# The shift of the first three layer norms computed by GpSimd instead of VectorE, in a decoder layer on one core

## The reference, cut to what matters

```python
def _layernorm(x, axis=-1, eps=1e-05):
    m = jnp.mean(x, axis=axis, keepdims=True)
    v = jnp.var(x, axis=axis, keepdims=True)
    return (x - m) / jnp.sqrt(v + eps)
...
    # end of _L0_xattn_ref: ln2, with a gain and an offset
    return layer_norm(att + decoder_seq, ln_gamma, ln_beta)
...
x = _layernorm(x + _L0_attn_ref(x, ...), axis=-1)             # ln1
x = _layernorm(x + _L0_xattn_ref(ctx_1024, x, ...), axis=-1)  # ln3 around ln2
x = _layernorm(x + _L0_ffn_ref(x, ...), axis=-1)              # ln4
```

## Time and profile before

| what | value |
|---|---|
| median of 3 runs | 441.6 us (441.42 to 441.95) |
| profiled execution, its own time | 443.31 us |
| its span from first to last instruction | 441.6 us |
| DVE busy over the span | 397.1 us (90%) |
| ACT busy | 340.6 us (77%) |
| PE busy | 274.4 us (62%) |
| POOL busy | 147.2 us (33%) |
| stretch of the three norms | 357.4 to 393.6 us of the span |

### The profile page before, as it was taken

The page is one execution under the profiler, slowest core; times in us unless marked ns, Lnnn a source line. Parts: engine busy times, 40 slices in busy tenths (PEclk is TensorE's granted clock), DMA queues, the critical chain, the costliest instruction groups (busy, mean ns, idle before and its releaser), DMA issues.

```text
span 441.6 us, 8251 instructions
## 1 busy us (share of the span) xinstructions
PE 274.4 (62%) x2265; PEld 150.6 (34%) x2275; DVE 397.1 (90%) x1261; ACT 340.6 (77%) x801; POOL 147.2 (33%) x327
## 2 busy tenths in 40 slices
PE   6777988989677733332332333399997886274560
PEld 5754435435222210000000000164444785161550
DVE  5978998778799999999999999959988988988987
ACT  2689985979999964999999999965796846548133
POOL 2400000001000000999999999992000005520020
PEclk9899998999755555555555555599999999579597
DMA  7700000000354441699998999877003200000002
GB/s 266 182 0 2 0 1 1 25 24 27 143 190 169 177 154 71 122 206 203 210 202 203 201 211 200 162 169 134 0 1 86 78 1 2 1 0 1 0 1 96
DMA packets 84254, 43.32 MB, mean 98 GB/s; under 512 B 69095, under 2 KB 74487, under 8 KB 84090
## 3 DMA queue, kind: packets, MB, share of 16 engines
q1 hardware_dynamic: 82650, 42.69, 38.5%
q10 hardware_dynamic: 1568, 0.21, 0.4%
HBM read 7.75 MB, written 1.58 MB: 21 GB/s over the span
## 4 chain that ended last, share of the span: by engine, by line
DVE 55%; PE 15%; issue 15%; ACT 11%; POOL 1%; DMA 1%; ACTq 0%; DVEq 0%; SPq 0%; POOLq 0%
DVE mem L1400 15%; PE ps L487 15%; DVE mem L1145 5%; DVE d_max L1148 5%; DVE mem L1315 3%; DVE mem L1572 3%; ACT mem L931 3%; ACT mem L967 2%; DVE r_now L1144 2%; DVE m L1715 2%; DVE m L1716 2%; DVE row_max L1400 2%; ACT mem L1003 2%; DVE neg_max L1144 2%; DVE m L1148 1%
## 5 line engine op out<-in xcount | busy, mean ns | idle before, releaser
L487 PE MATMUL ps<-mem 64*128 64x256 bf16 (+5 forms) x1180 | 173.7, 345 | 103.8 <-DVE row_max L1400 79.3
L487 PEld LDWEIGHTS ps<-mem 64*128 64x128 bf16 (+3 forms) x1188 | 66.2, 115 | 181.0 <-issue 65.9
L1003 ACT ACTIVATE mem<-mem,neg_max 128x256 f32<-128x256 int16 x256 | 118.2, 523 | 10.9 <-DVE neg_max L1144 8.6
L1400 DVE CUSTOM_DVE_ANT_0 mem<-ps,fold,c 128x256 int16<-128x256 f32 x256 | 108.7, 469 | 0.2 <-DVE fold L1145 0.2
L443 POOL TENSOR_SCALAR mem<-mem,r_now 128x256 int16<-128x256 f32 x176 | 82.0, 486 | 71.3 <-DVE r_now L1144 71.2
L487 PE MATMUL ps<-ones_bf 128*128 128x128 bf16 x766 | 60.6, 240 | 23.4 <-DVE m L1666 8.3
L487 PEld LDWEIGHTS ps<-ones_bf 128*128 128x128 bf16 x766 | 53.9, 109 | 40.0 <-ACT mem L967 11.5
L1315 DVE TENSOR_TENSOR mem<-mem 128x1024 bf16<-128x1024 bf16 x78 | 50.3, 694 | 4.4 <-ACT mem L931 3.0
L1003 ACT ACTIVATION_READ_ACCUMULATOR mem<-mem,neg_max x256 | 47.2, 184 | 0.0
L947 ACT ACTIVATE mem<-ps 128x1024 bf16<-128x1024 f32 x48 | 45.4, 1034 | 2.0 <-PE ps L487 1.0
L1148 DVE TENSOR_REDUCE d_max<-ps 128x1 f32<-128x1024 f32 (+1 forms) x33 | 38.1, 1161 | 2.6 <-PE ps L487 2.6
(11 more groups left out here) (218 smaller groups left out, 375.7 us busy)
## 6 DMA issues: line engine op xcount, KB each, us to landing
mem<-mem SPq DMA_DIRECT2D x64, 256.0 KB, 2.3
mem<-in_L_attn_w_qkv SPq DMA_DIRECT2D x1, 1536.0 KB, 8.7
mem<-in_x SPq DMA_DIRECT2D x4, 256.0 KB, 4.6
mem<-in_x SPq DMA_DIRECT2D x1, 1024.0 KB, 5.6
out<-mem SPq DMA_DIRECT2D x4, 256.0 KB, 2.2
xattn_matrix<-mem SPq DMA_DIRECT2D x1, 512.0 KB
mem<-in_L_attn_w_out SPq DMA_DIRECT2D x1, 512.0 KB, 4.6
mem<-in_L_ffn_W SPq DMA_DIRECT2D x2, 256.0 KB, 5.9
```

Of the source, the lines that this page charges most:

```text
L487: return te.matmul(o_, l_, r_, start=start, stop=stop)
L1003: ins = sc.activation(e_ring[:, u % 4, pos], y_ring[:, u % 4, pos], ACT.Exp, scale=scale_reg, bias=neg_max[:, u % 4, pos:pos + 1], accum_o ...
L1400: ins = ve.tensor_tensor_reduce(y_ring[:, unit % 4, pos], ps[:, bank + pos // 2, (pos % 2) * N:(pos % 2 + 1) * N], shift, col("g_dots"), - ...
```

## The change

The shift of ln1, ln2 and ln3 leaves DVE's list. POOL computes it, as two instructions of 128x4 with a semaphore between them: the product of mean and rsd, then times -1. The twelve pairs are put into POOL's list at the places below. DVE's norm steps, which had no wait of their own for rsd since the shift stood between, now wait for it. The fourth norm keeps its shift on DVE. Nothing else moves.

```diff
+            def rows_of(q):
+                return slice(4 * q, 4 * q + 4)
+
+            def shift_of(name, q):
+
+                pool.wait_ge(ln_sem(name, "rsd"), ln_count(name, q))
+                link(pl.tensor_tensor(nmr[:, rows_of(q)], mv[:, rows_of(q), 0], rsd[:, rows_of(q)], ALU.mult))
+                pl.tensor_scalar(nmr[:, rows_of(q)], nmr[:, rows_of(q)], -1.0, 0.0, ALU.mult, ALU.add)                    .then_inc(ln_sem(name, "shift"), 1)
...
-                    (x1_beta, 0), (x1_beta, 1), (x1_beta, 2), (gamma_n2, 0), (x1_beta, 3), (gamma_n2, 1),
-                    (gamma_n2, 2), (x2_b2, 0), (x2_b2, 1), (gamma_n2, 3), (x2_b2, 2), (x2_b2, 3)):
+                    (shift1, 0), (shift1, 1), (shift1, 2), (shift1, 3), (x1_beta, 0), (x1_beta, 1),
+                    (shift2, 0), (x1_beta, 2), (shift2, 1), (gamma_n2, 0), (x1_beta, 3), (gamma_n2, 1),
+                    (shift2, 2), (gamma_n2, 2), (shift3, 0), (shift2, 3), (x2_b2, 0), (shift3, 1),
+                    (gamma_n2, 3), (x2_b2, 1), (shift3, 2), (x2_b2, 2), (shift3, 3), (x2_b2, 3)):
...
             def normalise(name, dst, src, q, done):
+                dve.wait_ge(ln_sem(name, "rsd"), ln_count(name, q))
                 for t in range(4 * q, 4 * q + 2):
```

More of the change, by code:

```diff
@@ L449, in _, with shift1, shift2, shift3 @@
                 fine_unit(unit)
+            def rows_of(q):
[4 more added lines that the diff above has]
+                pl.tensor_scalar(nmr[:, rows_of(q)], nmr[:, rows_of(q)], -1.0, 0.0, ALU.mult, ALU.add)                    .then_inc(ln_sem(name, "shift"), 1)
+            def shift1(q):
+                shift_of("ln1", q)
+            def shift2(q):
+                shift_of("ln2", q)
+            def shift3(q):
+                shift_of("ln3", q)
             def x1_beta(q):
@@ L1626, in factor2 @@
                 factor("ln2", q)
[L1628 to L1635, removed]
             def shift4(q):
@@ L1670, in _ @@
                     (residual, 0), (residual, 1), (stats1, 0), (stats1, 1), (moments1, 0), (moments1, 1),
[L1671 to L1679, removed]
+                    (residual, 2), (factor1, 0), (factor1, 1), (stats1, 2),
+                    (residual, 3), (moments1, 2), (norm1, 0), (factor1, 2), (stats1, 3), (moments1, 3),
+                    (norm1, 1), (factor1, 3), (norm1, 2), (norm1, 3), (stats2, 0), (moments2, 0), (factor2, 0), (stats2, 1),
+                    (moments2, 1), (factor2, 1), (stats2, 2), (sum3, 0), (moments2, 2),
+                    (stats3, 0), (factor2, 2), (moments3, 0), (sum3, 1), (factor3, 0),
+                    (stats3, 1), (stats2, 3), (moments3, 1), (moments2, 3), (norm3, 0), (factor3, 1),
+                    (factor2, 3), (extremes, 0), (norm3, 1), (sum3, 2),
+                    (stats3, 2), (extremes, 1), (moments3, 2), (sum3, 3), (factor3, 2), (stats3, 3),
+                    (moments3, 3), (norm3, 2), (factor3, 3), (extremes, 2), (norm3, 3), (extremes, 3)):
                 step(q)
```

## The result

The changed kernel takes 447.92 us (447.69 to 448.07, 3 runs) against 441.60 (441.42 to 441.95): a ratio of 1.0141, 95% interval 1.0118 to 1.0164, so 1.4% slower. On another chip, where the kernel before came to 444.71, the ratio was 1.0091 (1.0059 to 1.0122).

| kernel | residual(0) starts | to the last extremes | on to the first gelu | from there to the end |
|---|---|---|---|---|
| before | 357.67 | 34.66 | 7.95 | 41.31 |
| after | 357.01 | 39.23 | 8.63 | 41.31 |
| after, second chip (e1_same_again) | 359.76 | 39.25 | 8.33 | 41.32 |

The account below looks back on a forecast made before the run. The prediction took a loop over DVE, ACT and POOL, not one full queue, to bound the kernel. +4.9 for the delayed last extremes and +0.3 for PE's clock made +5.2, so 446.8 us, range 444.5 to 448.4.

Parts of the forecast that it names:

- pair on POOL: The two shift instructions on POOL: 0.28 + 0.19 = 0.47 us, bounds 0.20 and 0.80.
- stats2(2), the one gain: ln2 on DVE: without the 0.69 us stall, stats2(2) starts at 373.55 instead of 373.76, a gain of 0.2 us.
- sum3(0) ends: DVE's sum3(0) waits until x1_beta(3) on POOL ends, and ends at 377.23 instead of 375.59: lag +1.6 us.
- ACT's norm3(0): ln3, quarter 0: shift3(0) queues behind gamma_n2(2) on POOL, so ACT's norm3(0) starts at 382.85 instead of 379.18: +3.7 us.
- ACT's norm3(1): ln3, quarter 1: shift3(1) queues behind x2_b2(0) on POOL, so ACT's norm3(1) starts at 386.9 instead of 382.37: +4.5 us.
- sum3(3) ends: DVE's sum3(3) needs gamma_n2(3), then x2_b2(1) holds the port: it ends at 392.3 instead of 387.78, +4.5 us.
- The queue's term: Up to the last extremes: shifts queued behind POOL's large instructions delay ACT's last norm3 and the last extremes by +4.9 us.
- The clock's term: PE's fold and first transposes: longer idle in front of the fold lowers the clock, +0.3 us, bounds 0 and 1.1.
- Rival A: sum3 and norm3 on DVE don't stall behind POOL, only the shifts' queueing remains: about +1.7, 443.3 us; chance 0.08.
- Rival B: POOL is free whenever rsd lands and DVE keeps its saved stalls: -1.6, 440.0 us; chance 0.06.
- the four moments named: When rsd for shift2(0), shift3(0), shift3(1) and shift3(3) lands: POOL must be neither in nor waiting before a large instruction.
- Rival C: No difference: queueing alone with a pair near 0.20 us, between -1.6 and +1.7, about 441.6 us; chance 0.06.

Follow-up runs that it names:

- e1_same_again: The changed kernel run once more, unaltered, on a second chip: 449.88 us against 444.71 for the kernel before, ratio 1.0091.
- e2: The changed kernel with shift3(0) moved ahead of gamma_n2(2), shift3(1) ahead of x2_b2(0), shift3(3) ahead of x2_b2(2) in POOL's list: ratio 1.0017 to the kernel before.
- e3: The changed kernel with the second instruction (times -1) of each pair left out, so its result is wrong: ratio 1.0042 to the kernel before.
- e5: The changed kernel with POOL waits: x1_beta(3) starts only after sum3(0), x2_b2(1) only after sum3(3): ratio 1.0109 to the kernel before.
- e11: The changed kernel, all twelve shifts on POOL, with the three lists reordered and the x2_b2 behind the first gelu: 438.33 us against 441.81 before.
- e9: The kernel before, all shifts on DVE, with the three lists reordered and the x2_b2 behind the first gelu: 438.04 us against 441.81 before.
- e8: Shifts of ln1 and ln3 on POOL, ln2's on DVE, three lists reordered, x2_b2 last in POOL's list: 438.94 us against 441.66 for the kernel before.
- e6: The changed kernel with only ln3's shifts on POOL, those of ln1 and ln2 back on DVE: ratio 1.0048 to the kernel before.

## Why the prediction was right

The time came out as forecast in sign and mechanism: 446.8 predicted, 447.92 measured, in the range of 444.5 to 448.4. By the trace the change costs 5.25 us against the 5.2 of the sum. The medians differ by 1.1 us more. That the span of before equalled its median did no harm, since the median plus 5.2 is 446.8 as well; the 1.1 us is in no stage from residual(0) on. The profiled execution of before, with 443.31 us, lay 1.7 us above its own median while the changed kernel's lay on it, so scatter ahead of residual(0) is the likely source. No trace of one of those three runs shows it, and on the second chip (5.2 by the medians, 5.0 by the traces) it is not there. The upper end of the range was not as worked out as it looks: 441.6 + 4.9 + 1.1 is 447.6, which the measured time exceeds, and the "few tenths" that make 448.4 of it are 0.8 us. That the time fell inside is partly luck.

Step by step, as lags against before measured from residual(0):

| step | reckoned | measured |
|---|---|---|
| pair on POOL | 0.47 us | 0.49 |
| start of ln2's first statistics | +0.37 | +0.28 |
| ACT's norm2(0), factor2(1) | +0.77 | +0.67, +0.67 |
| stats2(2), the one gain | -0.2 | -0.3 |
| sum3(0) ends | +1.6 | +1.5 |
| ACT's norm3(0) | +3.7 | +3.35 |
| extremes(0) | +1.9 | +1.6 |
| ACT's norm3(1) | +4.5 | +4.4 |
| sum3(3) ends | +4.5 | +4.4 |
| ACT's last norm3, last extremes | +4.9 | +4.6 |
| PE's clock | +0.3 (0 to 1.1) | +0.68, +0.38 |

The mechanism held at each step; e2 and e3 show that it is the queueing of the pairs, and not something beside it. Two terms were off in size. The queue's term was 0.3 too large, 0.1 of it from ln1, where the lag was 0.28 instead of 0.37. Between norm3(0) and the pair I took 0.2 for the port, and the row at 381.35 shows 0.20 for the instruction and no hold; but that was made up again at shift3(1), whose second instruction took 0.75 us instead of 0.19 beside DVE's sum3(2):

```profile
385.36 0.75 POOL L459 TENSOR_SCALAR mem<-mem 128x4 f32<-128x4 f32 x1
```

```profile
385.38 0.68 DVE L1656 TENSOR_TENSOR mem<-mem 128x512 f32<-128x512 f32 x1
```

Up to sum3(3) the reckoning is only 0.1 too large. The rest lies behind it: I put the end of x2_b2(2) at 395.6, and the trace has it at 395.35 on the same scale; the text of the reckoning doesn't say what I took there. The clock's term was off the other way: I took 0.3 because the 28 spare matmuls behind the fold would cover most of it. They did cover their own slowness (they ended at 402.5, when the transposes were due), but the fold, which stands ahead of that cover, took 0.52 us more; the rest is in the transposes behind. The two errors, -0.3 and +0.4, nearly cancel, and that the sum came within 0.05 us is luck. On the second chip, with the clock at +0.38, the sum of 5.2 is 0.2 too large.

Rival A (the queueing alone, +1.7) named as its sign that sum3 would be at 0.69; it was at 1.74. But e5 adds what the prediction only said in half a sentence: with sum3 let go by a wait on POOL the stretch is the same, so giving DVE the port first gains nothing there. Rival A's number assumed that neither queue waits for the other, which no order of the lists gave. Rival B (-1.6 if POOL is free whenever rsd lands) failed in the changed kernel at the four moments named; e2, which frees three of them, came to +0.75, and its first two pairs of ln2 still stand behind and ahead of large instructions. In e11 POOL is free at three of the four moments by order alone; shift2(0) still waits there behind x1_beta(1), from rsd at 367.87 to 369.20. Rival C needed a pair near 0.20 us, and the pair took 0.49.

## What to carry to other kernels

Ask of a moved instruction not only how long it takes, but what stands in front of it in the new queue at the moment its input lands, and what is queued behind its wait: an engine that is half idle can have no free moment where it counts. Parts of such a change don't add; +0.4 and +1.7 made +4.6, because the first part delays what the second is queued behind. A reckoning of all lists by hand, with durations from the profile, foretold the stretch of ten kernels within 0.7 us, and of one to 1.4 us, and is a way to find orders: the instructions of the kernel before in another order had a stretch 3.0 us shorter (e9), and those of the changed kernel one 8.5 us shorter (e11). The reckoning must reach past the stretch that it is to shorten: in e8 it ended there, and 1.8 us was lost just behind.

## What the runs showed of the hardware

A small instruction on GpSimd costs nearly the same for 4 elements as for 1 (0.20 and 0.19 us), and 0.29 from start to start with a semaphore between (0.28 for 1 element). In these traces DVE's stalls behind POOL hit instructions with two SBUF tensors and tensor_scalar on fp32 (norm3(0) 1.12 instead of 0.57 us, the fold's 2.30 instead of 0.48), never statistics (0.87 us for four) or reductions (0.67). It works the other way too: the second instruction of shift3(1) took 0.75 us at 385.36, and at 388.12 in the repeat e1.

Where POOL's large instructions follow each other, it matters on which side of the boundary DVE asks. The shift at 370.18 of the kernel before asked within the second of three and was done at 370.94, just behind that one's end at 370.91. sum3(0) of the changed kernel asked 0.08 us after x1_beta(3) had started and took 1.74 us instead of 0.69.

PE's clock after an idle stretch didn't follow from the length of the stretch alone: after 3.94 us idle the fold took 1.22 us at a granted clock of 0.50, after 4.59 us in e1 1.08 at 0.59, after 2.41 us in e3 1.01 at 0.65, but after 2.42 us in e8 and 2.67 us in e6 0.70 at 1.00.

```profile
394.72 1.01 PE L506 MATMUL ps<-fold,ones 128*128 128x256 f32 x2 [2.41 <-DVE fold L1164]
```

```profile
390.95 0.70 PE L506 MATMUL ps<-fold,ones 128*128 128x256 f32 x2 [2.42 <-DVE fold L1164]
```
